# Attention scores from two one-pass fp32 parts in two row halves of TensorE, with P.V in blocks

## The reference, cut to what matters

```
q = (x @ Wq.T + bq).reshape(b, s, HEADS, HEAD_DIM)
k = (x @ Wk.T + bk).reshape(b, s, HEADS, HEAD_DIM)
v = (x @ Wv.T + bv).reshape(b, s, HEADS, HEAD_DIM)
attn = jnp.einsum('bqhd,bkhd->bhqk', q, k) / np.sqrt(HEAD_DIM).astype(np.float32)
attn = jax.nn.softmax(attn, axis=-1)
attn = attn * head_mask[None, :, None, None]
out = jnp.einsum('bhqk,bkhd->bqhd', attn, v).reshape(b, s, HIDDEN)
return out @ Wo.T + bo
```

## Time and profile before

| | |
|---|---|
| median of 3 runs | 621.56 us (621.24 to 621.59) |
| span of the profiled execution, first to last instruction | 600.2 us |
| its own time | not given apart; the median stands 21.4 us above the span |
| TensorE, VectorE, ScalarE, GpSimd busy | 98%, 83%, 75%, 47% of the span |
| granted TensorE clock | 0.999 |
| attention stage | about 57 to 402 us |

### The profile page before, as it was taken

The page is one execution under the profiler, slowest core; times in us unless marked ns, Lnnn a source line. Parts: engine busy times, 40 slices in busy tenths (PEclk is TensorE's granted clock), DMA queues, the critical chain, the costliest instruction groups (busy, mean ns, idle before and its releaser), DMA issues.

```text
span 600.2 us, 21750 instructions
## 1 busy us (share of the span) xinstructions
PE 585.2 (98%) x8258; PEld 405.9 (68%) x8258; DVE 497.1 (83%) x1076; ACT 452.8 (75%) x967; POOL 280.1 (47%) x481
## 2 busy tenths in 40 slices
PE   6898999999999999999999999999999999999997
PEld 3443556555665655655655765656899999999966
DVE  8989999999999999999999999735577777777557
ACT  5887898888888888888888888985266555555551
POOL 7947430222542542542642642656745555555500
PEclk9999999999999999999999999999999999999999
DMA  6896333324434322322322311001422222222173
GB/s 177 224 303 208 110 80 93 102 79 121 126 91 128 90 57 61 85 57 64 82 57 66 82 56 47 21 20 49 93 56 67 70 70 70 71 70 70 42 294 136
DMA packets 43839, 57.66 MB, mean 96 GB/s; under 512 B 11130, under 2 KB 31482, under 8 KB 43754
## 3 DMA queue, kind: packets, MB, share of 16 engines
q1 hardware_dynamic: 39434, 47.59, 28.1%
q0 software_dynamic: 4320, 8.89, 4.6%
HBM read 35.76 MB, written 20.42 MB: 94 GB/s over the span
## 4 chain that ended last, share of the span: by engine, by line
PE 91%; ACT 3%; SPq 2%; DMA 1%; DVE 1%; issue 1%; POOL 0%; DVEq 0%; ACTq 0%
PE ps L1423 18%; PE ps L1451 18%; PE ps L1466 18%; PE ps L1677 11%; PE ps L1665 11%; PE ps L1624 4%; PE ps L1615 4%; PE ps L1405 2%; PE ps L1655 1%; PE ps L1486 1%; ACT xn L761 1%; PE ps L1411 1%; ACT probs L774 1%; PE ps L1497 1%; ACT probs L865 1%
## 5 line engine op out<-in xcount | busy, mean ns | idle before, releaser
L1002 DVE TENSOR_REDUCE mx<-ps 128x2 f32<-128x1024 f32 x256 | 306.2, 1212 | 20.2 <-PE ps L1423 12.2
L865 ACT ACTIVATE probs<-ps 128x512 f32<-128x512 f32 x512 | 296.8, 603 | 31.5 <-PE ps L1451 13.0
L1451 PE MATMUL ps<-q_op,k_op 128*32 128x512 bf16 x2048 | 205.0, 380 | 3.0 <-DMA q_op<-mxT 2.9
L1423 PE MATMUL ps<-k_op,q_op 96*32 96x512 bf16 x2048 | 161.0, 380 | 1.8 <-DVE mx L1002 1.3
L1466 PE MATMUL ps<-probs,v_op 128*32 128x256 f32 x2048 | 160.0, 378 | 0.0
L923 ACT ACTIVATE probs<-ps,b_cur 128x128 f32<-128x128 f32 x284 | 80.8, 368 | 59.4 <-PE ps L1665 58.6
L739 POOL DMA_INDIRECT results<-rest,row_id x71 | 71.6, 1009 | 66.5 <-DVE rest L1303 48.0
L1423 PEld LDWEIGHTS ps<-k_op,q_op 96*32 96x32 bf16 x2048 | 62.1, 97 | 52.9 <-DVE mx L1002 14.2
L1466 PEld LDWEIGHTS ps<-probs,v_op 128*32 128x32 f32 x2048 | 70.9, 109 | 38.7 <-ACT probs L865 0.2
L1451 PEld LDWEIGHTS ps<-q_op,k_op 128*32 128x32 bf16 x2048 | 64.5, 95 | 46.4 <-ACT probs L865 3.1
L630 POOL DMA_INDIRECT slots<-route_sb,slot_u x64 | 63.7, 995 | 58.0 <-ACT probs L865 49.7
(11 more groups left out here) (177 smaller groups left out, 543.0 us busy)
## 6 DMA issues: line engine op xcount, KB each, us to landing
q_op<-q_scr SPq DMA_DIRECT2D x96, 96.0 KB
k_op<-k_scr SPq DMA_DIRECT2D x96, 96.0 KB
w_sb<-in_W SPq DMA_DIRECT2D x18, 256.0 KB, 3.0
probs<-slots SPq DMA_DIRECT2D x71, 64.5 KB, 1.8
q_scr<-probs SPq DMA_DIRECT2D x8, 384.0 KB, 3.8
k_scr<-probs SPq DMA_DIRECT2D x8, 384.0 KB, 3.7
k_scr<-probs SPq DMA_DIRECT2D x8, 256.0 KB, 4.4
probs<-results SPq DMA_DIRECT2D x4, 512.0 KB, 4.8
```

The source lines that it names most:

```text
L865: nc.scalar.activation(probs[:, i, j, :], ps[:, BANK["key", b, hg, s], :], ACT.Exp, scale=float(D) ** -0.5).then_inc(s_exp, 1)
L1002: nc.vector.reduce_max(mx[:, slot % 2, 2 * p:2 * p + 2], ps[:, bank:bank + 2, :], AX.X).then_inc(s_max, 1)
L1423: last = nc.tensor.matmul(ps[c, BK_A + a % 4, :], q_op[hg][0:SH, j, P * i + c.start:P * i + c.stop], k_op[hg][0:SH, j, :], start=True, sto ...
L1451: last = nc.tensor.matmul(ps[c, bank, :], k_op[hg][:, j, P * i + c.start:P * i + c.stop], q_op[hg][:, j, :], start=True, stop=True)
```

## The change

- q and k are cut in two parts of fp32 type float32r (which TensorE multiplies in one pass), in place of three of bf16. ScalarE takes the first, VectorE subtracts it and writes the second; the second step on ScalarE and the one on GpSimd are gone. A head has 2 x 16 = 32 rows, and with one row of -1 (row scores) or three (key scores) 33 or 35.
- Two heads stand one in rows 0 to 63 and one in rows 64 to 127 of the operands. A tile of scores is one matmul of 128 columns and 512 moving columns on one half; two tiles follow each other, one on each half. A row pair is two heads now, where it was two query tiles of one head.
- Key scores come two tiles at a time, then the row pair. P.V comes in blocks of two key tiles (32 instructions in the records), in a group behind the row pairs 3 and 7 (`products`, PV_AT). The last two key tiles of a group are multiplied in the next group's first block.
- Maxima are transposed in fp32. `out_norm` begins one pair later; the projection stands one step later, other small jobs by one to three steps.
- Loads are 8 per group (16 rows x 2 heads x 2 KB) where they were 6 (24 rows x 4 heads x 1 KB); scratch is three sequences deep (DEEP). In the feed-forward stage the current weights and the read-back results lie in other buffers.

```
-PARTS = 3
+PARTS = 2
...
-SH = 96
+SH = KR + 1
...
-DEEP = 4
+DEEP = 3
...
-        PV_SLOTS = ((11, 12, 13, 15, 17, 19, 21, 23), (9, 11, 13, 15, 17, 19, 21, 23))
+        PV_AT = ((3, 3, 5, 5), (3, 3, 5, 5))
...
+        def head_of(s):
+
+            return s % 2 * JH + s % J // 2
...
-            def row_scores(b, hg, a):
-
-                j, i = a // NT, a % NT
-                if a == 0:
+            def row_scores(b, hg, p):
+
+                j, i, rows = p // NT, p % NT, KR + 1
+                if p == 0:
                     pe.wait_ge(s_ld[hg], (b + 1) * (16 * N_LD))
-                if a % 2 == 0:
-                    wait(pe, s_max, (b * HG + hg) * (J * NT // 2) + a // 2 - 1)
-                for c in QUARTERS:
-                    last = nc.tensor.matmul(ps[c, BK_A + a % 4, :], q_op[hg][0:SH, j, P * i + c.start:P * i + c.stop],
-                                            k_op[hg][0:SH, j, :], start=True, stop=True)
-                if a % 2:
-                    last.then_inc(s_sa, 1)
+                wait(pe, s_max, (b * HG + hg) * PAIRS + p - 1)
+                for half in range(2):
+                    at = ROW_HALF * half
+                    last = nc.tensor.matmul(ps[:, BK_A + 2 * (p % 2) + half, :], q_op[hg][at:at + rows, j, P * i:P * (i + 1)],
+                                            k_op[hg][at:at + rows, j, :], start=True, stop=True)
+                last.then_inc(s_sa, 1)
...
-                i, j = s // J, s % J
+                i, j, at, rows = s // J, head_of(s) % JH, ROW_HALF * (s % 2), SH + SHIFTS
...
-                for c in QUARTERS:
-                    last = nc.tensor.matmul(ps[c, bank, :], k_op[hg][:, j, P * i + c.start:P * i + c.stop], q_op[hg][:, j, :],
-                                            start=True, stop=True)
-                last.then_inc(s_sb, 1)
+                nc.tensor.matmul(ps[:, bank, :], k_op[hg][at:at + rows, j, P * i:P * (i + 1)], q_op[hg][at:at + rows, j, :],
+                                 start=True, stop=True).then_inc(s_sb, 1)
...
+            def products(b, hg, quad):
+
+                for i in range(NT):
+                    if PV_AT[(hg - 1) % 2][i] == NT + quad and b * HG + hg > 0:
+                        for half in range(2):
+                            pv((b * HG + hg - 1) // HG, (hg - 1) % HG, i, half)
+                for i in range(NT):
+                    if PV_AT[hg % 2][i] == quad:
+                        for half in range(2):
+                            pv(b, hg, i, half)
...
-                    for s in range(J * NT):
-                        key_scores(b, hg, s)
-                        if (b, hg, s) in ROWS:
-                            n = ROWS[b, hg, s]
-                            for a in (2 * (n % PAIRS), 2 * (n % PAIRS) + 1):
-                                row_scores(n // (HG * PAIRS), n // PAIRS % HG, a)
-                        for kind, *which in extras(b, hg, s):
+                    for s in range(0, J * NT, 2):
+                        both = (s, s + 1)
+                        for n in both:
+                            key_scores(b, hg, n)
+                        for n in both:
+                            if (b, hg, n) in ROWS:
+                                pair = ROWS[b, hg, n]
+                                row_scores(pair // (HG * PAIRS), pair // PAIRS % HG, pair % PAIRS)
+                        for kind, *which in extras(b, hg, s + 1):
                             if kind == "mx":
                                 max_rows(*which)
-                        for k in range(2 * NT):
-                            if PV_SLOTS[hg % 2][k] == s:
-                                pv(b, hg, k // 2, k % 2)
-                            elif PV_SLOTS[(hg - 1) % 2][k] == J * NT + s:
...
+                        if s % J == J - 2:
+                            products(b, hg, s // J)
```

More of the change, by code:

```diff
@@ L33 @@
 K_PARTS = 2 * PARTS - 1
+ROW_HALF = P // 2
+JH = J // 2
 SHIFTS = 2
-SH = 96
+SH = KR + 1
 E, F = 8, 512
@@ L100, in block_kernel @@
         xnT = sb("xnT", [P, 2, S])
-        qk32 = sb("qk32", [P, 2, 2, S])
+        w1_cur = sb("w1_cur", [P, TQ, F])
         rest = sb("rest", [P, 2, 2, S])
@@ L105, in block_kernel @@
         v_all = sb("v_all", [P, B, NT, C])
-        q_op = [sb(f"q_op{g}", [P, J, S], bf16) for g in range(HG)]
-        k_op = [sb(f"k_op{g}", [P, J, S], bf16) for g in range(HG)]
+        q_op = [sb(f"q_op{g}", [P, JH, S], f32r) for g in range(HG)]
+        k_op = [sb(f"k_op{g}", [P, JH, S], f32r) for g in range(HG)]
         v_op = sb("v_op", [P, HG, NT, J, 32])
-        mx = sb("mx", [P, 2, J * NT])
-        mx_parts = sb("mx_parts", [P, P], bf16)
-        mxT = sb("mxT", [SHIFTS * J * NT, 2, P], bf16)
+        mx = sb("mx", [P, 2, 2, JH * NT])
+        mx_parts = sb("mx_parts", [P, 2, SHIFTS, JH * NT])
+        mxT = sb("mxT", [SHIFTS * J * NT, 2, P], f32r)
         probs = sb("probs", [P, NT, J, S])
@@ L144, in block_kernel @@
         projected = rest[:, 0, 0, :]
-        parts = probs.rearrange("p i j s -> p (i j s)").bitcast(bf16)[:, 2 * J * S:2 * J * S + DEEP * 2 * PARTS * S]
+        parts = probs[:, 1:1 + DEEP, :, :].rearrange("p i j s -> p (i j s)")
         parts = parts.rearrange("p (u w k s) -> p u w k s", u=DEEP, w=2, k=PARTS)
@@ L1171, in attend @@
                             last_max_out()
-                        if 3 <= p < 7 and hg == 2:
-                            out_norm(b, 0, p - 3)
-                        elif 3 <= p < 7 and hg == 0 and not first:
-                            out_norm(b - 1, 1, p - 3)
+                        if p >= 4 and hg == 2:
+                            out_norm(b, 0, p - 4)
+                        elif p >= 4 and hg == 0 and not first:
+                            out_norm(b - 1, 1, p - 4)
                         if not first:
@@ L1600, in _ @@
             sequences(attend)
-            for k in range(2 * NT):
-                if PV_SLOTS[(HG - 1) % 2][k] >= J * NT:
-                    pv(B - 1, HG - 1, k // 2, k % 2)
+            for i in range(NT):
+                if PV_AT[(HG - 1) % 2][i] >= NT:
+                    for half in range(2):
+                        pv(B - 1, HG - 1, i, half)
             pe.wait_ge(s_wffn, 16 * N_WFFN)
```

139 lines of the change are left out of this document (54 added, 85 removed).

## The result

| | kernel before | the change |
|---|---|---|
| median of the runs | 621.4 us (620.3 to 621.59) | 777.6 us (771.94 to 780.19, 4 runs) |
| span of the profiled execution | 600.2 us | 774.7 us |
| granted TensorE clock, mean | 0.999 | 0.791 |

The ratio is 1.25, with a 95% interval of 1.2447 to 1.2552: 25% slower, where 644 us (606 to 672) were forecast. The direction was right, the size far off.

A forecast was written before the change was run, and what follows sets the result against it. TensorE was taken to pace the attention stage; blocked P.V then leaves a slower waiting loop: +21.8, +2.5 in the last groups, -2 for the split. Span 600.2 becomes 622.5, plus 21.4 gives 644 us, range 606 to 672.

The forecast's parts named there:

- (c), the clock: Rival: TensorE's clock falls to 1.2 GHz for half the attention stage, +75 us, 720 us; chance 0.03.
- The hand-over loop: Attention stage: ScalarE idles about 1.6 us across each P.V block; eight tiles take 5.48 us for 5.20, +2.9 per sequence.
- Mode change, 0.25 us for both ways: TensorE switching between row halves and P.V's column quarters: 0.14 in, 0.11 out; a P.V block becomes 1.98 us.
- The dearer price: Alternative cost of switching tiling around P.V: estimated 0.17 us per drain, 0.33 per block, total 5 us longer.
- A row pair at 0.22, halves side by side: Score matmuls: two tiles, one on each half of the array, run together in 0.22 us.
- rival (a): Array halves not side by side: 657 us, chance 0.16; fp32 also at 0.43 per tile: 850, chance 0.04.
- Rival (b), the faster side: Attention stage: ScalarE and VectorE bridge the P.V block, 42 us per sequence, 599 us; chance 0.24 including anything up to today.
- Split, -2: Cutting q and k before the attention stage: fewer ScalarE and GpSimd parts, larger stores; -2 us, bounds -4 and +5.
- The 21.4 us outside the span: Median of runs, 621.56, lies 21.4 us above the profiled span; carried over unchanged to the forecast.

The follow-up runs named there:

- x1_order: Kernel before with only the change's order (key tiles in twos, P.V in blocks, small jobs moved), bf16 column quarters kept: 653.6 us, ratio 1.050.
- x11_before35: Kernel before with bf16 score matmuls contracting 35 rows instead of 96 and 128, exponential's scale an eighth: 842 to 1010 us, ratio 1.36.
- x3_double: The change with every score matmul issued twice, same operands and target: 737 us (one run).
- x9_early: The change with exact 64-row halves, P.V spread as in the kernel before and output normalisation steps moved back earlier: 622.2 us, ratio 0.999 to the kernel before.
- x4_rows64: The change with score matmuls on all 64 rows of each half instead of 33 or 35, exponential's scale an eighth: 674.1 us (one run).

## Why the prediction was right or wrong

- **The step that failed is (c), the clock:** "I don't expect it to fall", with a chance of 0.03, read from a row of the first 15 us; the sum then gave the clock no term at all. The row is true, and the change shows 1.00 there again. But its matmuls contract 128 rows, and it says nothing of matmuls on 33 and 35. Instead the clock averaged 0.791, at 0.5 to 0.8 through the attention stage. Going from 35 to 64 rows per half gives back 103 us of the 156. What is left, 674.1 against 621.4, is nearer to the forecast than to the result. The price that I named, 720 for half the stage at half clock, points the right way.
- The page of the Trainium skill that I cited there, "TensorE: Matmul & The Clock Gate", A second HAM failure mode, blames micro-idles between groups of matmuls. The runs show that they aren't enough and aren't needed: x1_order has more idle time than the change and holds 0.999, x11_before35 falls to 0.50 with none. They may still have a part in the change, since x3_double, with the gaps filled and the rows as few, is back at 0.96.
- **The direction** was right, and not by luck alone: the loop that I forecast is there and costs 31 us. But it is a fifth of what was measured.
- **The hand-over loop was right in mechanism and a little small.** I had "+2.9" per sequence, +22 in all; the order alone gives +31, and 49.9 us per sequence against 46.1 in the kernel before profiled again, +3.8. ScalarE's idle stretch (1.62 for "about 1.6") and the pace of eight tiles are as worked out. Short were the start of the first exponential (0.55 for 0.47) and VectorE's steps on the output, which hold back a row pair; how the rest divides isn't shown.
- **Mode change, 0.25 us for both ways:** right where the scores stay in quarters (0.24 in x11_before35), short with row halves. There the round of x9_early pays 0.34, since the first pair behind P.V takes 0.34 and not 0.23. The dearer price that I worked out from the Trainium skill, "TensorE: Matmul & The Clock Gate", Single matmul latency, an estimated 0.33, is the nearer one for this form.
- **A row pair at 0.22, halves side by side:** right in a burst, 2 x 0.114 = 0.23, so rival (a) falls. In the kernel it is 0.33 to 0.34 next to P.V.
- **Rival (b), the faster side,** did not come in this order. With P.V spread and the clock up, a sequence takes 44.8 us, for 46.1 in the kernel before profiled again, but also for 44.8 in the faster execution that the earlier trace rows come from. The whole kernel ties.
- **Split, -2:** nothing of it was gained. The first key scores start at 52.5 us in the change and at 51.7 in the kernel before profiled again.
- **The 21.4 us outside the span:** wrong as a reading. In the sum it did no harm, since only a difference was added to the median; but the pace of 44.79 us per sequence was that of an unusually fast execution.

Step by step the way from 621 to 778 is: order +31 (x1_order), row halves with 64 rows in that order +21 (x4_rows64, one run, its clock still at 0.967), 35 rows for 64 +103.

## What to carry to other kernels

A granted clock read in one stretch says nothing sure of another form of matmul. When a change halves the rows that a matmul contracts, TensorE may be as busy as before and be granted half the clock, so price both levels before anything else. A burst of the new form is a weak test, because it has none of the kernel's gaps: the change's own form, both halves in turn on 35 rows, stayed at 1.00 in its burst. Nor does one good stretch settle it: x11_before35 ran at full clock for some 150 us and at half clock before and after. The surer test is the whole kernel with the new number of rows and nothing else changed.

If rows are left over, fill them with zeros. A matmul on 64 rows takes as long as one on 35 (0.114 us in turn on 35, 11.00 / 94 = 0.117 on 64), and here this gave 103 us; the exact version pays about 3 us for clearing the shift rows. And a shape that packs better pays at every change of shape, so count the changes per round before the savings.

## What was not expected of the hardware

- Half clock with TensorE busy throughout, on 35 rows: 52.00 of 52.00 us at 1.00 and 90.00 of 90.00 at 0.50, same program, same kernel (x11_before35).
- Added work that makes a kernel faster: every score matmul twice, 777.6 to 737 us, with the clock at 0.96 (one run).
- A matmul over all 128 rows before one on a half holds the engine 0.43 us instead of 0.23.
- The start of the program ran at 0.80 in some executions and at 1.00 in others of the same kernel (0 to 15 us), without a matching difference in time.
